# Half of the prologue's pieces in the second turn, loads in another order with W in two pieces, and the choice's intermediate values in PSUM

## Time and profile before

| what | value |
|---|---|
| time, median of 3 runs | 1929.82 us (1928.17 to 1935.44) |
| profiled execution | 1931.39 us |
| its span | 1929.6 us, mean granted clock 0.957 |
| busy share PE, DVE, ACT, POOL | 90%, 79%, 71%, 71% |
| start of turn 1's scan on POOL | 156.6 us |
| experts from | 1515.7 us |

### The profile page before, as it was taken

The page is one execution under the profiler, slowest core; times in us unless marked ns, Lnnn a source line. Parts: engine busy times, 40 slices in busy tenths (PEclk is TensorE's granted clock), DMA queues, the critical chain, the costliest instruction groups (busy, mean ns, idle before and its releaser), DMA issues. The chain is left out here.

```text
span 1929.6 us, 34291 instructions
## 1 busy us (share of the span) xinstructions
PE 1737.9 (90%) x12348; PEld 1498.9 (78%) x12348; DVE 1532.0 (79%) x3109; ACT 1374.2 (71%) x2699; POOL 1372.7 (71%) x644
## 2 busy tenths in 40 slices
PE   5778999999999999999999999997656699999997
PEld 4556787887878888788887888876555588899996
DVE  1547888888888888888888888889999577766663
ACT  3368889888888888888888888886432555666663
POOL 0007899898999989899898998989776145454442
PEclk9898999999999999999999999998786799999998
DMA  4003222232221322323223222232212254455552
GB/s 188 1 2 88 62 71 64 63 63 87 64 72 57 72 84 48 86 62 72 78 40 95 66 67 71 52 84 76 50 41 64 77 131 129 128 135 132 132 133 23
DMA packets 120744, 149.88 MB, mean 78 GB/s; under 512 B 8192, under 2 KB 111104, under 8 KB 120320
## 3 DMA queue, kind: packets, MB, share of 16 engines
q1 hardware_dynamic: 108288, 130.91, 24.4%
q0 software_dynamic: 12288, 16.79, 4.9%
HBM read 121.98 MB, written 17.30 MB: 72 GB/s over the span
## 5 line engine op out<-in xcount | busy, mean ns | idle before, releaser
L1166 POOL TENSOR_TENSOR room<-room 128x1024 f32<-128x1024 f32 x256 | 606.1, 2368 | 199.5 <-DVE room L1081 156.2
L1147 DVE TENSOR_TENSOR_SCAN room<-pD,last,room 128x256 f32<-128x256 f32 x1024 | 691.6, 732 | 49.3 <-PE pD L1098 38.3
L1156 POOL TENSOR_TENSOR room<-room 128x1024 f32<-128x1024 f32 x256 | 606.3, 2368 | 95.8 <-PE pY L1115 85.3
L1128 ACT ACTIVATE room<-room,fixed,kkT 128x512 f32<-128x512 f32 x512 | 406.5, 806 | 82.5 <-PE pD L1098 80.5
L1098 PE MATMUL pD<-fixed,room 128*128 128x128 f32 x2048 | 323.6, 282 | 83.7 <-DVE room L1147 79.7
L1098 PEld LDWEIGHTS pD<-fixed,room 128*128 128x128 f32 x2048 | 247.1, 146 | 114.3 <-issue 74.5
L1115 PE MATMUL pY<-fixed,room 128*128 128x128 f32 x2048 | 322.8, 282 | 4.3 <-POOL room L1156 4.3
L1115 PEld LDWEIGHTS pY<-fixed,room 128*128 128x128 f32 x2048 | 253.9, 147 | 53.1 <-issue 26.0
L323 POOL DMA_INDIRECT xg<-xn_rows,W x64 | 68.0, 1063 | 207.4 <-DVE W L317 192.5
L1719 ACT ACTIVATE h<-ph 128x512 f32<-128x512 f32 x128 | 76.6, 599 | 140.9 <-PE ph L1749 97.5
L1749 PE MATMUL po<-w_up,h_up 128*128 128x256 f32 x512 | 148.6, 290 | 0.4 <-DVE h_rest L1639 0.3
(11 more groups left out here) (282 smaller groups left out, 3651.5 us busy)
## 6 DMA issues: line engine op xcount, KB each, us to landing
room<-kq_rows SPq DMA_DIRECT2D x256, 256.0 KB, 5.3
w_in<-w_d SPq DMA_DIRECT2D x32, 1024.0 KB
room<-ndS SPq DMA_DIRECT2D x16, 512.0 KB, 3.3
xt<-x_in SPq DMA_DIRECT2D x16, 256.0 KB, 3.0
y_out<-xo SPq DMA_DIRECT2D x16, 256.0 KB, 2.1
xn_rows<-xnC SPq DMA_DIRECT2D x16, 256.0 KB, 2.1
W<-weights SPq DMA_DIRECT2D x1, 3505.5 KB, 13.5
room<-wmod SPq DMA_DIRECT2D x1, 1536.0 KB, 20.8
```

The costliest lines, as they stand in the source:

```text
L1128: act.activation(decT[:, m % 2, t, :], turn2(ndT, it, NT * DI, t * DI, DI), ACT.Identity, bias=ones_s[:, 0:1], scale=turn2(kkT, it, NT * D ...
L1147: dve.tensor_tensor_scan(run, pD[h][:, k2 * TB:(k2 + 1) * TB], run, last[:, bass.ds(later(it) * (DS * DT) + m * DT + k, 1)], ALU.mult, ALU ...
L1156: pool.tensor_tensor(sq[:, m % 2], st[:, m % 4], kqb[:, m % SLOTS, 1, :].unsqueeze(1).broadcast_to([P, DT, TB]), ALU.mult).then_inc(sem("r ...
L1166: pool.tensor_tensor(st[:, m % 4], turn2(u, it, DT * TB).rearrange("p (k t) -> p k t", k=DT), kqb[:, m % SLOTS, 0, :].unsqueeze(1).broadca ...
```

## The change

1. Loads: x block 1 goes second, ahead of wmod0. W goes in two pieces: columns up to "win2" (3616, semaphore `weights_in`), then, behind the rest of wmod0 and folds, the others (`weights2_in`). PE waits for `weights_in` at its first low-rank product instead of ahead of turn -1, PE and ACT for `weights2_in` at turn 0.
2. DVE's reading of the first mod columns and the copy of `causal` move from ahead of turn -1 to its steps 2 and 4; ACT waits for `tail0` at the first modulate.
3. Prologue pieces: gate rows g from steps 14, 28, 36, 44 of turn -1 to steps 12, 18 of turn -1 and 5, 20 of turn 0; the bias parts, b1s and dskip from 50 to 56 to steps 5 to 8 of turn 0; oproj_g from 58 to step 30 of turn 0. `early` is awaited at turn 1. Block 1's relu and FFN product wait for `tail0` 4 (b1s).
4. Choice: bitsu, step, red, a column of ones and two scratch tiles a and b lie in the bank behind the sums. Every elementwise instruction on two tensors, and the copies, get an operand there. The token copy goes to ACT, `value_part` goes ahead of `look`, and bitsu is copied for each list.
5. kk is made as k * -1 * kT with k from PSUM.

```diff
-EARLY_CONSTS = SEL_AT["bitsu"][0]
+EARLY_CONSTS = SEL_AT["prob"][0]
+BANK_AT, _ = layout([("sums", P), ("bitsu", 3 * LOOKS), ("step", 1), ("one", 1), ("red", TT), ("a", P), ("b", P)])
...
     def act_exp(self, act, b):
         act.wait_ge(self.sem("centred"), b + 1)
+        at = slice(b * LB, (b + 1) * LB)
+        act.activation(self.value[:, 0:2, at], self.token[:, :, at], ACT.Copy)
...
+        def scratch(name, dt=F32):
+            a, w = BANK_AT[name]
+            return bank[:, a:a + w] if dt == F32 else bank[:, a:a + w].bitcast(dt)
+
+        bitsu, step, red = scratch("bitsu", U32), scratch("step", U32), scratch("red")
...
-            do(dve.tensor_tensor(cand, thr.broadcast_to([P, 3]), self.bitsu[:, i * 3:i * 3 + 3], ALU.bitwise_or))
+            do(dve.tensor_tensor(cand, thr.broadcast_to([P, 3]), bitsu[:, i * 3:i * 3 + 3], ALU.bitwise_or))
...
-                do(dve.tensor_reduce(self.step, self.passed, AX_X, ALU.add))
-            do(dve.tensor_tensor(thr, thr, self.step, ALU.bitwise_or))
+                do(dve.tensor_reduce(step, self.passed, AX_X, ALU.add))
+            do(dve.tensor_tensor(thr, thr, step, ALU.bitwise_or))
...
         def value_part(n):
...
+            part, value = scratch("a"), self.value[:, :, at]
+            if n < 3:
+                do(dve.tensor_copy(value[:, 2 + n, :], part))
+            if n < 2:
+                do(dve.tensor_tensor(part, part, value[:, 2 + n, :], ALU.subtract))
...
+            do(dve.tensor_tensor(scratch("a").rearrange("p (e t) -> p e t", t=TT), prob.rearrange("p t e -> p e t"),
+                                 red.unsqueeze(1).broadcast_to([P, E, TT]), ALU.mult))
+            dve.tensor_copy(self.pl[:, at], scratch("a")).then_inc(sem("selected"), 1)
...
+            run, kept = scratch("b"), scratch("a")
+            dve.tensor_tensor_scan(run, scratch("one").broadcast_to([P, P]), equal, 0.0, ALU.mult, ALU.add)
...
+            posi, loi, hi = scratch("a", I32), scratch("b", I32), scratch("a")
...
-                dve.tensor_tensor(kk[:, :, :], kT[:, :, :], kT[:, :, :], ALU.mult).then_inc(sem("kk"), 1)
+                dve.scalar_tensor_tensor(kk[:, :, :], k_of, -1.0, kT[:, :, :], ALU.mult, ALU.mult).then_inc(sem("kk"), 1)
...
             for half in range(2):
+                if (it, half, n) == (1, 0, AT["relu0"]):
+                    act.wait_ge(sem("tail0"), 4)
...
+        MODS_AT, ROWS_AT, OUT_AT = (18, 24), (12, 18, STEPS + 5, STEPS + 20), STEPS + 30
+        FOLDS_AT = (34, STEPS + 5, STEPS + 6, STEPS + 7, STEPS + 8)
...
-            if isinstance(i, int) and i == 0:
+            if i == 0:
+                pe.wait_ge(sem("weights2_in"), 16)
+            if i == 1:
                 pe.wait_ge(sem("early"), 1)
             for n in range(STEPS):
-                if isinstance(i, int) and i == -1:
-                    early_pe(pe, n)
+                if i < 1:
+                    early_pe(pe, n + (i + 1) * STEPS)
...
-                sp.dma_start(W[:, :], weights).then_inc(sem("weights_in"), 16)
+                first = WEIGHT_AT["win2"][0]
+                sp.dma_start(W[:, 0:first], weights[:, 0:first]).then_inc(sem("weights_in"), 16)
...
+                sp.dma_start(W[:, first:], weights[:, first:]).then_inc(sem("weights2_in"), 16)
```

More of the change, by code:

```diff
@@ L139 @@
 SEL_TILES = [("samelist", P, F32), ("segbefore", P, F32), ("iota", P, F32), ("token", 2 * LT, F32), ("bitsf", 3 * LOOKS, F32),
[L140 to L143, removed]
+             ("prob", LB, F32), ("pl", LT, F32), ("seg", P, F32),
+             ("hit", 3 * P, F32), ("run", P, F32), ("value", PARTS * LT // 2, BF16), ("thr", 1, U32),
+             ("cand", 3, U32), ("cnt", 3, F32), ("passed", 3, F32), ("offset", 1, F32), ("need", 1, F32),
+             ("lo", LT, F32), ("quarter", SL * LT // 2, BF16),
              ("entries", 2 * TT * PARTS * SL // 2, BF16), ("onehot", 2 * TT * P // 2, BF16), ("gates", NL * SL, F32),
@@ L242, in dve_step @@
             dve.wait_ge(sem("scores"), (b + 1) * BPB + 1)
[L243 to L248, removed]
+            do(dve.tensor_reduce(red, sc, AX_X, ALU.max))
+            dve.tensor_tensor(sc, sc, red.unsqueeze(2).broadcast_to([P, TT, E]), ALU.subtract).then_inc(sem("centred"), 1)
+            dve.wait_ge(sem("const2_in"), 16)
+            dve.tensor_copy(bitsu, self.bitsf)
+            dve.memset(scratch("one"), 1.0)
             do(dve.memset(thr, 0))
@@ L567, in modulate @@
             act.wait_ge(sem(f"turn_{n}"), it + 1)
+            if (it, n) == (1, "a"):
+                act.wait_ge(sem("tail0"), 3)
             for c in range(DC):
@@ L687, in attn_pe @@
             if n == AT["wo"]:
+                if it == 1:
+                    pe.wait_ge(sem("folded"), 1 + B)
                 pe.wait_ge(sem("og"), it + 1)
@@ L876, in front_pe @@
             if n == AT["wout"]:
+                if it == 1:
+                    pe.wait_ge(sem("tail0"), 4)
                 pe.wait_ge(sem("facc"), (it + 1) * FJ)
@@ L1274, in early_pe @@
                 mod_cols(pe, 0, MODS[1]).then_inc(sem("modcols"), 1)
-            for half, at in enumerate((18, 24)):
+            for half, at in enumerate(MODS_AT):
                 if n == at:
@@ L1282, in early_pe @@
                         i.then_inc(sem("modcols"), 1)
-            for g, at in enumerate((14, 28, 36, 44)):
+            for g, at in enumerate(ROWS_AT):
                 if n == at:
@@ L1295, in early_act @@
         def early_act(act, n):
-            for g, at in enumerate((16, 30, 38, 46)):
-                if n == at:
+            for g, at in enumerate(ROWS_AT):
+                if n == at + 2:
                     act.wait_ge(sem("rows"), g + 1)
@@ L1311, in plus_one @@
                 dve.tensor_scalar(at, at, 1.0, None, ALU.add)
+            if n == 2:
+                mod_read(dve, 1, 0, MODS[0])
+                dve.wait_ge(sem("cols"), 1)
+                at = col0[:, DC * B:2 * DC * B]
+                dve.tensor_scalar(at, at, 1.0, None, ALU.add).then_inc(sem("tail0"), 1)
             if n == 4:
+                dve.wait_ge(sem("fixed_in"), 16)
+                dve.tensor_copy(causal[:, :], fx("causal"))
+                dve.wait_ge(sem("silc"), 2)
                 for layer in range(2):
@@ L1322, in early_dve @@
                 plus_one(col0, 4)
-            if n == 26:
+            if n == MODS_AT[1] + 2:
                 mod_read(dve, 3, 1, MODS[0])
@@ L1328, in early_dve @@
                 plus_one(col1, 4)
-            for g, at in enumerate((18, 32, 40, 48)):
-                if n == at:
+            for g, at in enumerate(ROWS_AT):
+                if n == at + 4:
                     dve.wait_ge(sem("gabs"), g + 1)
@@ L1350, in early_dve @@
                     dve.tensor_tensor(bg[:, b, :], fo("bout"), gb0, ALU.mult).then_inc(sem("folded"), 1)
-            for part, at in enumerate((50, 52, 54)):
+            for part, at in enumerate(FOLDS_AT[1:4]):
                 if n == at:
@@ L1359, in early_dve @@
                     dve.tensor_tensor(bg[:, :, :], bg[:, :, :], bpart[:, :, :], ALU.subtract).then_inc(sem("folded"), 1)
-            if n == 56:
-                dve.scalar_tensor_tensor(b1s[:, :], w("w1"), w("bin"), w("b1"), ALU.mult, ALU.add)
+            if n == FOLDS_AT[4]:
+                dve.scalar_tensor_tensor(b1s[:, :], w("w1"), w("bin"), w("b1"), ALU.mult, ALU.add).then_inc(sem("tail0"), 1)
                 for k in range(DT):
                     dve.tensor_scalar(dskip[:, k, :], fx("ident"), w("dskip")[:, k:k + 1], None, ALU.mult)
-            if n == 58:
+            if n == OUT_AT:
                 dve.wait_ge(sem("grows"), 9)
@@ L1421, in turn_act @@
             a, f, s, c, g = blocks_of(i, stages)
-            if isinstance(i, int) and i == 0:
+            if i == 0:
+                act.wait_ge(sem("weights2_in"), 16)
+            if i == 1:
                 act.wait_ge(sem("early"), 1)
             for n in range(STEPS):
-                if isinstance(i, int) and i == -1:
-                    early_act(act, n)
+                if i < 1:
+                    early_act(act, n + (i + 1) * STEPS)
                 for it, m in ((c, n + STEPS), (s, n), (f, n - STEPS)):
@@ L1445, in turn_dve @@
             for n in range(STEPS):
-                if isinstance(i, int) and i == -1:
-                    early_dve(dve, n)
+                if i < 1:
+                    early_dve(dve, n + (i + 1) * STEPS)
                 for it, m in ((c, n + STEPS), (s, n), (f, n - STEPS)):
@@ L1562, in _ @@
                 act.preload_act_table_set("natural_log_exp_and_others")
-                act.wait_ge(sem("tail0"), 3)
+                act.wait_ge(sem("tail0"), 2)
                 pipeline(act, turn_act)
```

72 lines of the change are left out of this document (27 added, 45 removed).

## The result

| what | before | after |
|---|---|---|
| time, median | 1932.05 us (1928.17 to 1935.44, 4 runs) | 1876.15 us (1875.84 to 1876.97, 4 runs) |
| span of the profiled execution | 1929.6 us | 1875.2 us |
| mean granted clock | 0.957 | 0.972 |
| first product on POOL | 156.6 us | 141.9 us |
| experts from | 1515.7 us | 1461.3 us |

A forecast was written before the change was run, and what follows sets the result against it. Dependent steps were taken to bound the first turns, PE the steady turns, DVE the last two stretches. From 1931.4: start -10.7, choice -26.7, kk 0, second choice +1.5 gave 1895.5, so 1894 us; own range 1885 to 1904, 8 in 10 1882 to 1914.

The forecast's parts named there:

- The 3 to 5 us that might have stayed: First list's choice: part of the 26.7 us gain that would stay if new scans and copies still waited for POOL.
- with a steady turn's share of gaps: Last two stretches: POOL sets the time and keeps steady-turn gaps, giving about 80.5 and 87.6 us, -26.7 in sum.
- if POOL's gaps all vanish: Last two stretches: the far bound on the choice's gain, -38 us.
- the start: First two turns, up to POOL's first product: loads and moved pieces save 10.7 us (-14 to -3).
- The loads: Ahead of turn -1: 1697.5 KB of W come later, so DVE's first statistics come 4.0 us earlier.
- the fourth rows and keys1: Turn -1: the rows leave PE ahead of q1, -2.7 us; keys1 no longer waits behind grows and bias parts, -2.5.
- the removed bias parts: End of turn -1: bias parts, b1s and dskip are gone before the last states; output product L678 gains 0.4 us.
- Turn 0: Second turn, which takes the moved pieces: costs +1.7 us, bounds 0 and +8.
- The second choice: List block 1's choice, in the experts: value parts, small PSUM operands and ACT's token copy cost +1.5 us (0 to +4).
- My 60 ns: DVE's choice instructions: an operand in PSUM costs some 0.06 us more each, 4 us of DVE work a list.
- Halved: Last turns: PE's low clock holds them, the stretches give -4 and -10 instead of -26.7, time 1907; chance 0.17.
- The slower rival: Start of the experts: 1.2 GHz granted for longer; gain gone from 36 us, 1946 us with two lists; chance 0.03.

The follow-up runs named there:

- The run with two tiles put back: The changed kernel with two small tiles of the choice, bitsu and step, in SBUF again: 1908.61 us, ratio 0.9886.
- The run with less work for PE: The changed kernel with the attention's gate projection summed over only half its inputs in all 16 blocks: 1872.98 us, ratio 0.9689.
- The run of the choice alone: The kernel of before with part 4 of the change only: 1892.61 us, ratio 0.9788.
- the run with less work on POOL: The changed kernel with 8 of the last block's 16 POOL products by q cut to half their columns: 1869.85 us, ratio 0.9668.
- the start alone: The kernel of before with parts 1 to 3 of the change only: 1915.93 us, ratio 0.9912.
- kk alone: The kernel of before with only kk (L1069) taking k from PSUM: 1932.63 us, ratio 1.0008.
- more of the start moved: The changed kernel with mod columns, gate rows and fold moved later, layer 1's columns to steps 12 and 14 of turn 0: 1880.19 us, ratio 0.9731.

## Why the prediction was right or wrong

**Right: the cause.** DVE's small instructions with two SBUF tensors wait for POOL's product, those with an operand in PSUM do not, and this was the bound of the last turns. The run with two tiles put back shows it by itself. In one reading the prediction went too far: not each of the small instructions of before ended with a product of POOL, but 21 of the 30. The rule of the Trainium skill ("SBUF — State Buffer", section "Who interferes with whom"), that one engine holds the shared pair for a whole instruction and that a DVE instruction with at most one SBUF input, outside the two-port modes, does not need it, agrees with these traces down to the forms that no row of before had: the scan (432 ns) and the copies out of the bank (293). The 3 to 5 us that might have stayed did not.

**Wrong: "with a steady turn's share of gaps".** This step gave POOL the gaps of a steady turn in both stretches, and made 80.5 and 87.6 us, 168.1 in all, of which 154.8 are POOL's work. (Neither figure follows from the 6.9 us of gaps named: 75.5 + 6.9 is 82.4, and the share of 6.9 in 74.6 makes 7.3 us for 79.1, and not 8.5. The two slips all but cancel, 168.8 for 168.1.) Measured, from the same start to the same distance behind POOL's last product, it is 157.4. POOL's gaps there are about 2 us, and not 13. In a steady turn they are not POOL's own: PE is busy 78.8 of 81.5 us and hands the sums out late (4.0 us of waits), and the turn's length leaves the rest. The last turns have no attention: PE has 378 instructions instead of 593, and once DVE is free next to nothing stands between POOL and its 64 products. That the missing attention is the reason is read from these rows; no run puts PE's work back. The run with less work for PE agrees: 0.9 us less for PE took 0.4 us of POOL's gaps out of a steady turn. The right term was the other bound that I had written beside it, -38 "if POOL's gaps all vanish"; -37.4 came. The run of the choice alone has 154.5 us with 154.07 of POOL, and the run with less work on POOL shortens the stretch. I had a row to choose by: in the earlier trace rows PE has 64.5 us of work in the stretch of 88.1, so a steady turn's cause of gaps was absent. The same term held the lower end of the range at 1882: it went down to -34 for the choice and -13 for the start, and both came out beyond (-37.4 and -14.8).

**Wrong in size: the start, -14.8 and not -10.7.** In the five profiles whose start is that of after, POOL's first product lies between 141.7 and 143.4 us, 13.2 to 14.9 earlier than before, so all are beyond the forecast. The loads (-4.4 for -4.0) and the second half of the chain held: between the two L588 it is 5.9 us less, 5.2 being forecast for the fourth rows and keys1; up to the first one 2.2 less for 2.8. Two terms look off:
- After the second L588 I gave 0.4 us to the removed bias parts. In the trace of before S (L807) starts at 75.72, 4.4 us behind the transposes; in after it is 2.5, which is the -1.9. Half of it is DVE's: the eight products that S needs (L598) end at 74.80, and DVE is at dskip for another 0.9 us. The other half is PE's: these products take 2.08 us, at a granted clock of 0.50 from 72.2 to 75.6, and 1.16 in after.
- Turn 0 was to cost +1.7 and gave 0.4; in the second profile of the changed kernel it costs 1.2. The pieces did what the steps said: the third rows stand ahead of the transposes (1.89 us), and the bias parts fit into DVE's idle time with 0.95 us left. But products that were there before became shorter: the eight of wo 2.87 to 1.97 us, the four transposes 1.11 to 0.60. The granted clock goes with it: 0.86 before and 0.98 after from 60 to 80 us, 0.83 and 1.00 from 100 to 120. In the second profile it is 0.91 from 60 to 80 us, the eight of wo take 3.35 us, longer than before, and the transposes 0.60 again. So that the clock helped by itself in the one profile is luck, as far as these runs tell. I had costed PE's pieces by their own durations and left the others as they were.

**Right: kk.** 0 was forecast and -1.8 measured over 14 turns, but none of it is shown to be kk's: the start alone, with kk in SBUF, has the same 1138.3 us for these turns as after. 1.4 of the 1.8 is the one turn of before in which the clock fell at 888 us. The turns of 81.79 and 81.84 occur in before, the choice alone and kk alone, and in no run with the new loads; why stays open. That PE sets the turns is shown by the run with less PE work for its first 0.4 us; that DVE is half a us behind was not in the forecast.

**The second choice.** +1.5 was forecast, and the experts are as long as they were. For instructions on two tensors an operand in the bank costs nothing that matters: 159 ns in after for 164 in the earlier trace rows, 156 for 160, kk 180 for 182. My 60 ns came from L220 against L222, which are two different operations, and so did the agreement that I saw with the Trainium skill's figure ("VectorE: DVE Perf Modes", section "The TRN2 errata", an estimate of 65 ns for a PSUM source): in instructions that read one tensor from each, no run here shows it. In instructions on a single tensor it is there: the same cast takes 232 ns from SBUF in the second list of before and 293 from the bank (L290 above), and the integer instruction on L284 agrees (228 from SBUF, 299 in the bank).
```profile
L285 DVE CAST W<-W 128x128 f32<-128x128 int32 x1 | 0.2, 232 | 0.0
```
There are too few of these to be seen in the time.

**The rivals.** "Halved" rested on POOL's 20.8 us of waits for PE at a low clock. They are 0.9 us in the last turn of after, and came back at 19.9 when only DVE's operands were put back; the clock rose too, from 0.73 to 0.80 and 0.84 to 0.93, with the same number of products (387 and 378) in less time. The slower rival found no support: the experts begin with 12 products in 5.29 us for 5.38 in the earlier trace rows, and the fast ones follow.

## What to carry to other kernels

When the engine that sets a stretch is freed, do not give the next in line the gaps that it has elsewhere: ask who makes those gaps, and whether that work is in this stretch. If not, take its busy time as the length. Small DVE instructions beside long POOL products are to be read by their mean durations in two places, one with POOL busy and one with it idle; one PSUM operand for two tiny tiles was worth 30 us here. A piece moved off a chain should go into a place where its engine waits: two columns in the chain of turn 0 came with 10 to 11 us there, one column beside it with 1 to 2. And before a term of one or two us is explained, look at a second profile of the same kernel: here the same first two turns ended 1.6 us apart, and those of before and of the choice alone 5.5.

## What was not expected of the hardware

- One operand in PSUM and one in SBUF is no slower on DVE than two in SBUF: 159 against 164 ns, 180 against 182.
- The wait is longer than the instruction by a factor of ten: a mean of 1660 ns for three numbers, up to about the 2366 ns of one POOL product.
- On a single 128x128 tensor the bank does cost: 292 to 300 ns where the same forms have 223 to 232 from SBUF.
- The changed kernel's runs lie within 1.1 and 1.6 us of each other on two occasions, those of before between 1926.65 and 1942.69 us. It is not the bank alone: the other kernels with the whole choice there spread over 4.0 to 6.4 us.
- A single fall of the granted clock to 0.50 for 3.4 us, at 888 us in before and 893 in the choice alone, stands in the one steady turn that is 1.4 us longer than the rest. The other profiles have none in the 13 steady turns.
- PE's products of turn 0 ran at many durations from profile to profile: the eight of wo took 2.87 us in before, 3.38 in the choice alone, 1.97 and 3.35 in the two profiles of the changed kernel, 3.65 with more of the start moved, with the granted clock of turn 0's stretches of 20 us between 0.59 and 1.00. What decides it stays open.
